# The second cross attention of a perceiver block: context loaded with features over partitions, root and shift spread by transfers

## The reference

```python
def layernorm(t, g, b):
    mu = jnp.mean(t, axis=-1, keepdims=True)
    var = jnp.var(t, axis=-1, keepdims=True)
    return (t - mu) * jax.lax.rsqrt(var + EPS) * g + b
xn = layernorm(x, ln_x_g, ln_x_b)             # x: the context
ln = layernorm(latents, ln_l_g, ln_l_b)
q = ln @ Wq
kv = jnp.concatenate((xn, ln), axis=1) @ Wkv
k, v = jnp.split(kv, 2, axis=-1)
q, k, v = (heads(q) * scale, heads(k), heads(v))
sim = jnp.einsum('bhid,bhjd->bhij', q, k)
sim = jnp.where(mask_full[:, None, None, :], sim, max_neg)
attn = jax.nn.softmax(sim.astype(jnp.float32), axis=-1).astype(sim.dtype)
out = jnp.einsum('bhij,bhjd->bhid', attn, v)
```

## Time and profile before

| | |
|---|---|
| Median of 3 runs | 2112.92 us (2111.11 to 2114.09) |
| The profiled execution | 2115.48 us |
| its span in the profile | 2113.3 us |
| TensorE busy | 1977.3 us, 94% |
| VectorE busy | 1569.6 us, 74% |
| ScalarE busy | 1044.0 us, 49% |
| GpSimd busy | 657.6 us, 31% |
| Mean DMA rate | 50 GB/s |

### The profile page before, as it was taken

The page is one execution under the profiler, slowest core; times in us unless marked ns, Lnnn a source line. Parts: engine busy times, 40 slices in busy tenths (PEclk is TensorE's granted clock), DMA queues, the critical chain, the costliest instruction groups (busy, mean ns, idle before and its releaser), DMA issues. The chain is left out here.

```text
span 2113.3 us, 45029 instructions
## 1 busy us (share of the span) xinstructions
PE 1977.3 (94%) x18290; PEld 1103.7 (52%) x18290; DVE 1569.6 (74%) x2777; ACT 1044.0 (49%) x1484; POOL 657.6 (31%) x696
## 2 busy tenths in 40 slices
PE   7899999999789788999999999999999999888998
PEld 3455555555555443455555555555555555544643
DVE  4689999999857673677777777777777776654676
ACT  2689998998813542333333333333333333323453
POOL 3244444454412230133333322333333322313100
PEclk9899999999799899999999999999999999999999
DMA  4323323322133210000000000000000000210300
GB/s 149 103 54 99 93 65 95 97 64 72 31 142 116 108 41 22 22 23 23 23 4 20 23 23 23 23 23 23 23 2 23 23 23 2 81 46 0 145 21 20
DMA packets 39613, 106.22 MB, mean 50 GB/s; under 512 B 19312, under 2 KB 21616, under 8 KB 33264
## 3 DMA queue, kind: packets, MB, share of 16 engines
q1 hardware_dynamic: 39408, 103.35, 16.1%
HBM read 75.42 MB, written 1.05 MB: 36 GB/s over the span
## 5 line engine op out<-in xcount | busy, mean ns | idle before, releaser
L1468 POOL TENSOR_SCALAR a1c_p_hi<-a1c_pf 128x512 f16<-128x512 f32 x272 | 201.1, 740 | 666.6 <-ACT a1c_pf L1524 624.1
L1326 PE MATMUL PS<-a_x_hi,w_next 128*128 128x512 f16 x1088 | 280.9, 381 | 3.8 <-DVE a1c_v_lo L1598 1.7
L1336 PE MATMUL PS<-w_next,a_x_hi 128*128 128x512 f16 x1088 | 279.0, 379 | 0.0
L1493 ACT ACTIVATE a1c_k_hi<-PS 128x512 f16<-128x512 f32 x136 | 81.2, 597 | 329.4 <-PE PS L1326 329.4
L375 POOL TENSOR_SCALAR a0c_p_hi<-a0c_r 128x1024 f16<-128x1024 f32 x128 | 154.9, 1210 | 268.7 <-DVE a0c_r L475 265.8
L1500 ACT ACTIVATE a1c_v_hi<-PS 128x512 f16<-128x512 f32 x136 | 81.6, 600 | 258.8 <-PE PS L1336 206.0
L480 DVE TENSOR_TENSOR a0c_p_lo<-a0c_r,a0c_p_hi 128x1024 f16<-128x1024 f32 x128 | 201.8, 1576 | 0.9 <-POOL a0c_p_hi L375 0.9
L1673 DVE TENSOR_TENSOR a1c_p_lo<-a1c_pf,a1c_p_hi 128x512 f16<-128x512 f32 x272 | 197.8, 729 | 6.0 <-POOL a1c_p_hi L1468 6.0
L1524 ACT ACTIVATE a1c_pf<-PS,a_maskc 128x512 f32<-128x512 f32 x256 | 175.1, 686 | 49.0 <-PE PS L1835 39.0
L1616 DVE CUSTOM_DVE_ANT_0 a1c_junk<-PS,a1c_maskr 128x512 bf16<-128x512 f32 x256 | 175.9, 687 | 18.8 <-DVE a1c_ctop L1616 0.5
L475 DVE TENSOR_TENSOR a0c_r<-PS,a0c_r 128x1024 f32<-128x1024 f32 x128 | 155.4, 1214 | 32.8 <-ACT a0c_r L421 32.6
(11 more groups left out here) (368 smaller groups left out, 4606.3 us busy)
## 6 DMA issues: line engine op xcount, KB each, us to landing
a_cf<-in_ctxT SPq DMA_DIRECT2D x16, 1024.0 KB, 5.2
a0c_ks<-a0c_k_hi SPq DMA_DIRECT2D x128, 128.0 KB, 2.3
a1c_cf<-in_ctx SPq DMA_DIRECT2D x16, 1024.0 KB, 4.8
a0c_ks<-a0c_k_lo SPq DMA_DIRECT2D x64, 128.0 KB, 2.3
f_w<-in_w SPq DMA_DIRECT2D x4, 1024.0 KB, 8.2
f_w<-in_w SPq DMA_DIRECT2D x1, 4096.0 KB, 20.2
qw_raw<-in_w_gate SPq DMA_DIRECT2D x1, 2816.0 KB, 10.3
qw_raw<-in_w_up SPq DMA_DIRECT2D x1, 2816.0 KB, 11.2
```

The lines of the kernel that those rows point to most:

```text
L1326: mm = nc.tensor.matmul(out, wk[i][:, k, f * P:(f + 1) * P], (x_hi, x_lo)[j][e][:, k, :], start=(step == 0), stop=(step == 11))
L1336: mm = nc.tensor.matmul(out, (x_hi, x_lo)[j][e][:, k, t * P:(t + 1) * P], wv[i][:, k, group * BANK:(group + 1) * BANK], start=(step == 0), ...
L1468: nc.gpsimd.tensor_scalar(p_hi[:, v % 4, :], pf[:, v % 2, :], 1.0, 0.0, ALU.mult, ALU.add)\
```

## The change

The context chunk is now loaded twice: once as before with rows over partitions (`cf`), only for the moments, and once from the transposed copy that the first layer reads too, with *features* over partitions (`ct`, 1 MB, L1406 of the changed file). In `ct` the root and the shift of the normalisation belong to columns, so they have to stand on every partition: SP writes the 2 x 512 numbers `rn` to HBM (`rows_out`, elements of 4 bytes), waits, and reads them back to all 128 partitions (`rows`). VectorE then computes ct x gx x rstd and adds gx x nmr in two instructions for each 128 features (`context_norm`), ScalarE adds the bias and writes the high half `x_hi` directly, VectorE the low half. The transposes, GpSimd's normalising and its high halves are gone; the ring loses its places for the transposes. Moments move to units 1, 2, 4, 5, root and Newton step to unit 6; in the start they move into units 3 to 8.

```diff
-    TURN = UNITS - KT - 1
+    MADE = UNITS - KT - 1
-            if TURN <= v < TURN + KT and j < NCH:
-                RING_ORDER.append(("turn", j, v - TURN))
...
                         if c >= 1:
-                            sp.wait_ge(turned, 4 * c)
+                            sp.wait_ge(stats_done, NT * c)
...
+                        if c >= 1:
+                            sp.wait_ge(x_lo_done, KT * c)
+                        sp.dma_start(ct[:].rearrange("p k n -> p (k n)"), d["ctxT"][c]).then_inc(ct_in, 16)
+
+                    def spread_rows(c):
+
+                        if c >= NCH:
+                            return
+                        sp.wait_ge(newton, 5 * (c + 1))
+                        sp.dma_start(rows_out[c % 2].rearrange("a (t p) -> p a t", p=P), rn[:], allow_slow_non_contiguous=True)\
+                            .then_inc(rows_kept, 16)
+                        sp.wait_ge(rows_kept, 16 * (c + 1))
+                        if c >= 1:
+                            sp.wait_ge(x_done, KT * c)
+                        sp.dma_start(rows[:].rearrange("p a n -> p (a n)"),
+                                     rows_out[c % 2:c % 2 + 1].rearrange("o a n -> o (a n)").broadcast_to([P, 2 * CH]))\
+                            .then_inc(rows_in, 16)
 
...
                     load_context(0)
                     tops(0, 0)
+                    spread_rows(0)
                     load_context(1)
                     for j in range(NJ):
                         tops(j, 1)
+                        spread_rows(j + 1)
                         tops(j + 1, 0)
                         load_context(j + 2)
...
-                    def normalise(c):
-
-                        pool.wait_ge(newton, 5 * (c + 1))
-                        for t in range(NT):
-                            nc.gpsimd.tensor_scalar(cf[:, t, :], cf[:, t, :], rstd[:, t:t + 1], nmr[:, t:t + 1],
-                                                    ALU.mult, ALU.add).then_inc(z_done, 1)
...
-                    normalise(0)
                     mask_row(0)
-                    for k in range(KT):
-                        context_hi(0, k)
...
-                            if j + 1 < NCH and v == 9:
-                                normalise(j + 1)
                             if j + 1 < NCH and v == 11:
                                 mask_row(j + 1)
-                            if j + 1 < NCH and v > TURN:
-                                context_hi(j + 1, v - TURN - 1)
...
-                    def context_f32(c, k):
-                        act.wait_ge(turned, KT * c + k + 1)
-                        if c >= 1 or k >= 2:
-                            act.wait_ge(x_lo_done, KT * c + k - 1)
-                        nc.scalar.activation(xf[:, k % 2, :], g.PS[:, ring_bank("turn", c, k), :], ACT.Identity,
-                                             bias=bx[:, k:k + 1], scale=gx[:, k:k + 1]).then_inc(x_done, 1)
+                    def context_hi(c, k):
+                        act.wait_ge(x_done, KT * c + k + 1)
+                        if c >= 1:
+                            act.wait_ge(v_product, 8 * c)
+                        nc.scalar.activation(x_hi[(c + 1) % 2][:, k, :], ct[:, k, :], ACT.Identity,
+                                             bias=bx[:, k:k + 1]).then_inc(x_hi_done, 1)
...
-                    inverse_root(0)
                     for v in range(UNITS):
                         evacuate(0, v)
-                        if TURN <= v < TURN + KT:
-                            context_f32(0, v - TURN)
+                        if v == 7:
+                            inverse_root(0)
+                        if MADE <= v < MADE + KT:
+                            context_hi(0, v - MADE)
                     for j in range(NJ):
                         for v in range(UNITS):
                             if j + 1 < NJ and v >= 1:
                                 evacuate(j + 1, v - 1)
-                            if j + 1 < NCH and v > TURN:
-                                context_f32(j + 1, v - TURN - 1)
+                            if j + 1 < NCH and MADE <= v < MADE + KT:
+                                context_hi(j + 1, v - MADE)
                             probability(j, v)
-                            if j + 1 < NCH and v == 8:
+                            if j + 1 < NCH and v == 6:
                                 inverse_root(j + 1)
...
-                            dve.wait_ge(z_done, NT * c)
+                            dve.wait_ge(rows_kept, 16 * c)
...
+                    def context_norm(c, k):
+
+                        if k == 0:
+                            dve.wait_ge(ct_in, 16 * (c + 1))
+                            dve.wait_ge(rows_in, 16 * (c + 1))
+                        nc.vector.scalar_tensor_tensor(out=ct[:, k, :], in0=ct[:, k, :], scalar=gx[:, k:k + 1],
+                                                       in1=rows[:, 0, :], op0=ALU.mult, op1=ALU.mult)\
+                            .then_inc(x_scaled, 1)
+                        dve.wait_ge(x_scaled, KT * c + k + 1)
+                        nc.vector.scalar_tensor_tensor(out=ct[:, k, :], in0=rows[:, 1, :], scalar=gx[:, k:k + 1],
+                                                       in1=ct[:, k, :], op0=ALU.mult, op1=ALU.add).then_inc(x_done, 1)
 
                     def context_lo(c, k):
                         dve.wait_ge(x_hi_done, KT * c + k + 1)
                         e = (c + 1) % 2
-                        nc.vector.tensor_tensor(x_lo[e][:, k, :], xf[:, k % 2, :], x_hi[e][:, k, :], ALU.subtract)\
+                        nc.vector.scalar_tensor_tensor(out=x_lo[e][:, k, :], in0=ct[:, k, :], scalar=bx[:, k:k + 1],
+                                                       in1=x_hi[e][:, k, :], op0=ALU.add, op1=ALU.subtract)\
                             .then_inc(x_lo_done, 1)
+
+                    def context_step(c, v):
+
+                        if MADE <= v < MADE + KT:
+                            context_norm(c, v - MADE)
+                        if MADE < v <= MADE + KT:
+                            context_lo(c, v - MADE - 1)
...
-                    for t in range(NT):
-                        moments(0, t)
-                    newton_step(0)
                     for v in range(UNITS):
                         if v >= 1:
                             split_lo(0, v - 1)
+                        if 3 <= v < 3 + NT:
+                            moments(0, v - 3)
+                        if v == 8:
+                            newton_step(0)
                         if v % 2 == 0 and v >= 2:
                             after_period(0, v // 2)
                         if v == 11:
                             new_diag(0, 0)
-                        if v > TURN:
-                            context_lo(0, v - TURN - 1)
+                        context_step(0, v)
...
-                            if j + 1 < NCH and v in (1, 3, 5, 7):
-                                moments(j + 1, (1, 3, 5, 7).index(v))
-                            if j + 1 < NCH and v == 8:
+                            if j + 1 < NCH and v in (1, 2, 4, 5):
+                                moments(j + 1, (1, 2, 4, 5).index(v))
+                            if j + 1 < NCH and v == 6:
                                 newton_step(j + 1)
-                            if j + 1 < NCH and v > TURN:
-                                context_lo(j + 1, v - TURN - 1)
+                            if j + 1 < NCH:
+                                context_step(j + 1, v)
...
-                    def turn(c, k):
-                        bank = ring_bank("turn", c, k)
-                        freed("turn", c, k)
-                        if k == 0:
-                            pe.wait_ge(z_done, NT * (c + 1))
-                        for t in range(NT):
-                            mm = nc.tensor.transpose(g.PS[:, bank, t * P:(t + 1) * P],
-                                                     cf[:, t, k * P:(k + 1) * P], g.ident[:])
-                        mm.then_inc(turned, 1)
...
-                        if TURN <= v < TURN + KT and j < NCH:
-                            turn(j, v - TURN)
```

25 lines of the change are left out of this document (10 added, 15 removed).

## The result

The changed kernel takes **2223.41 us** (median of 4 runs, 2219.51 to 2229.66) against 2113.51 us before (4 runs, 2111.11 to 2117.97): ratio 1.0503, 95% interval 1.0461 to 1.0545. The forecast was 2207 us, range 2168 to 2245. Direction and mechanism came as forecast, the time 16 us higher. The profiled execution of the changed kernel took 2219.51 us with a span of 2217.7, so its span is 104.4 us longer than before, where the prediction said 93.7.

The account below looks back on a forecast made before the run. TensorE, busy 94% of the span, was taken as the bound. Span: 2113.3 - 26.6 - 4.0 + 96.3 + 1.0 + 27 = 2207.0 us, +93.7; on the median 2112.92 that gives 2207 us, range 2168 to 2245.

Parts of the forecast that it names:

- transposes gone, a turn: TensorE in the loop: removing four groups of transposes a chunk saves 1.77 us a turn, 26.6 us in all.
- stall without clock, a turn: TensorE idle ahead of scores 12 (2.7 us) and scores 14 (3.7 us): 6.4 us a turn, 96.3 us in fifteen.
- clock, a turn: Half clock after TensorE's two new pauses: 1.8 us a turn, 27 us in all, bounds 0 to 51 us.
- start, to the first scores: Ahead of the loop: old pause, half clock and transposes go, VectorE waits 2.4 us for rows; gain 4.0 us.
- What bounds the kernel: In the loop TensorE alone sets the 59.54 us turn; what leaves it leaves the time if nobody becomes late.
- Where it lies: VectorE steps 11 to 14: exponentials queue on ScalarE behind context_hi, which waits for context_norm; 6.4 us of stall a turn.
- The price of `context_norm`: On VectorE: two instructions at 0.69 and 0.73 us, 1.42 us until the result is there.
- The rival without loss of clock: TensorE's loop pauses come but the clock stays full: 2180 us; chance 0.20.
- the removal is simply gained: Rival: exponential 11 ends by 7.2 us and the others likewise, so no loop stall: 2082 us; chance 0.06.
- Transfers: SP's write and read-back of root and shift, under 9 us with the issues, stay hidden: cost 0.
- The slack of 15.8 us: Time in a turn from the end of the small steps until VectorE needs the rows: 15.8 us.
- Dearer VectorE: Rival: all eight new VectorE instructions at 0.89 us lengthen the chain 1.6 us a turn: 2231 us; chance 0.11.

Follow-up runs that it names:

- experiment 1: Changed kernel with ScalarE's context_hi moved behind the exponential of the same unit, nothing else: 2179.06 us.
- experiment 7: Changed kernel with context_hi on GpSimd, earlier start, loop moments in units 1 to 4, root and Newton step in 5, context_norm in 10 to 13: 2094.99 us.
- experiment 5: Changed kernel with context_hi made by GpSimd instead of ScalarE, its mask row moved from unit 11 to 10: 2132.34 us.
- experiment 3: Changed kernel with root and shift written as 128 pieces of 32 bytes, context_norm reading and writing at a 32-byte stride: 2260.76 us.
- experiment 8: Changed kernel without context_norm's second instruction, so the shift is not added: 2183.95 us.
- experiment 4: Changed kernel with 40 unused 128x128 products on TensorE ahead of scores 12 and of scores 14: 2205.68 us.
- experiment 2: Kernel before, transposes kept, plus eight VectorE instructions a turn on spare data at context_norm's places, nobody waiting for them: 2140.86 us.
- experiment 6: Changed kernel with an earlier start only: moments in units 1 to 4, root 5, Newton step 6, rows sent ahead of first tops: 2221.10 us.

## Why the prediction was right, and where it was off

Measured against its own sum, all from the two profiled executions (us):

| term | predicted | measured |
|---|---|---|
| transposes gone, a turn | -1.77 | -1.75 |
| stall without clock, a turn | +6.42 | +6.99 |
| clock, a turn | +1.8 | +1.33 |
| late diagonal, a turn | 0 | +0.23 |
| pair 0-1, a turn | 0 | +0.08 |
| fifteen turns (with 1.0 for the first in the forecast) | +97.7 | +103.1 |
| start, to the first scores | -4.0 | +2.2 |
| last two turns | 0 | -2.3 |
| behind the loop | 0 | +1.5 |
| span | +93.7 | +104.4 |

The sum is nearer than its terms, and that is partly luck: the stall came 8.6 us dearer than forecast and the late diagonal 3.4, the clock 7 us cheaper, and the last two turns gave 2.3 back. The largest single miss is the start, 6.2 us and the wrong sign.

*What bounds the kernel.* Right: TensorE set the turn before, and the removal of the transposes is worth 1.75 us a turn when nothing else gets late. The pair 10-11 of experiment 1 shows it (7.23 us with the transposes gone). Experiment 7 realises it: its eight pairs add to 58.5 us on average against 59.47 before, with 0.7 us of new delay left in the last.

*Where it lies.* Right, and the core of the case. Against scores 10 as 0, exponential 11 was put at 9.87 and ended at 10.03, exponential 13 at 20.83 and ended at 21.65, exponential 15 at 27.91 and ended at 28.77. Scores 0 were said to need no wait, and had none. That ScalarE's order is the cause is shown by experiment 1 (move it: 44 us back), experiment 5 (take it off ScalarE: 91 us back, same load on VectorE) and experiments 3 and 8 (make `context_norm` longer or shorter by 3.1 and about 3 us a turn: the turn follows by 3.3 and 2.8).

*The price of `context_norm`.* Mis-sized. The two instructions take 0.746 and 0.752 us and give their result 1.53 us after they begin (1384.58 to 1386.11), not 0.69, 0.73 and 1.42. `context_hi` takes 0.72, not 0.69. Four blocks of this make the 0.57 us by which the stall without clock exceeds its forecast, 8.6 us in fifteen turns. The nearest row was p_lo, a tensor_tensor. It is the operation that makes the difference, not the type: `context_lo` was a tensor_tensor in f32 and f16 of 0.68 us and is now, with the same types, a scalar_tensor_tensor (L1596) of 0.747 us. The low half of the values is a scalar_tensor_tensor too, but reads one operand from PSUM, and takes 0.69 (1387.97).

*The clock.* Right in kind, too large in size: 1.33 against 1.8 us a turn. Both pauses (2.79 and 2.75 us in the turn shown) were put on the same side as those of the earlier trace rows, of 2.61 and 2.56 us. The granted clock fell around the first in thirteen of the fifteen turns, around the second in nine, so not behind every pause. The pair 12-13 is between 11.36 and 11.92 us, the pair 14-15 between 7.22 and 9.52. The rival without loss of clock, 2180 us, is out by experiment 4.

*What VectorE's load does by itself.* Not in the prediction at all. It judged VectorE by who waits at the scores, and said for the rival *the removal is simply gained* that only step 11 and context_hi decide it. Experiment 2 shows a second path, through the PSUM ring and the low half of the values, which costs 25 us with nobody waiting for the new results. In the changed kernel it is hidden, since TensorE stands at the scores anyway; it came out in experiment 2 and, smaller, in experiment 7. So 2082 us could not have been reached without moving VectorE's work too.

*Transfers.* No turn waits for the rows, as forecast, but the step to it was wrong, and the cost is not zero. The write was priced at 2.0 us, the row of a 256 KB output, and takes 9.2 in the start; SP's waits on it average 9.9 us (138.6 / 14). The total was to be under 9 us and is about 14 with the read of 4.4. The slack of 15.8 us (worked out from the start of the last small step, not its end; the write in fact left SP 10.08 us before scores 10) covered that, but not the `tops` behind it: the prediction let them need SP only from -2.5 us on, and by then SP was to be free. It is held until up to 2.4 us after scores 10, and the diagonal waits. Pair 10-11 is 0.23 us a turn over its 10.07, 3.4 us in fifteen, of which 0.8 come from turn 4, where TensorE itself stood for 0.54 us among its score products without a wait that the profile shows. The Trainium skill ("DMA: Bandwidth & Descriptors", Rules for kernel authors) says that a pattern whose last dimension is not contiguous becomes one descriptor for each element, which here would be 1024 a turn. That fits: the page of the changed kernel counts 60861 packets against 39613 before, and in experiment 3, with 128 pieces a turn, 46525. The 14336 fewer are just 16 x (1024 - 128). Experiment 3 shows the pieces to be the cause: 128 pieces of 32 bytes for the same 4 KB land in 1.4 to 1.7 us. Whether their number or their size counts is not separated.

*The start.* Wrong in sign. The step that failed is the wait of 2.4 us for the rows, since it rested on the 2.0 us write; it was 10.01 us, and brought the half clock back that the prediction had counted as gained. With the rows earlier, experiments 6 and 7 start the scores at 869.31 and 866.42 us, 4.6 and 7.5 us ahead of the kernel before: the gain of 4.0 us (forecast bound 7.4) is there once the write is paid early.

*The last two turns.* They gave 2.3 us back, for which the forecast had nothing. The 2.56 us pause of the earlier trace rows at 1834 is 1.04 us after the change. Before, the diagonal ahead of it had waited for the maxima's transfer:

```profile
1832.25 1.04 DVE L1372 TENSOR_TENSOR a1c_diag<-a_ident,a1c_topx 128x512 bf16<-128x512 bf16 x1 [1.55 <-DMA a1c_topx<-a1c_topb]
```

After, it waits 0.37 us, and the half clock that followed the longer pause is gone. Why that transfer landed earlier is open.

*Dearer VectorE.* Did not happen to `context_norm` in the changed kernel, for the reason given (GpSimd's pass follows the exponential and meets other instructions). It happened to the last `context_lo` of fourteen chunks, 1.10 us beside a GpSimd pass, but TensorE was not waiting there. In experiments 1 and 5 it fell on the path.

## What to carry over

Before you move work to an engine, ask who waits for it *in order*, and what is queued behind the waiter: here a result that takes 1.5 us, on an engine with 26% of its time free, cost 5% of the kernel, because the conversion that needed it stood in the same list as the exponentials on which TensorE depends. Moving it one place back in that list gave 44 us, taking it out of the list 91. Place the consumer on an engine in whose queue nothing urgent stands behind it, or make the producer so early that the wait is never met, and check both ends: after that repair the next wait was at the last block's deadline, and after that at the PSUM ring. A transfer of a few KB in a thousand pieces is not a small transfer; price it by its pieces, and ask the same question of it: what is queued behind it.

## What the hardware showed that I had not expected

- A write of 4 KB from SBUF to HBM in 1024 pieces of 4 bytes takes 8.8 to 11.5 us in the changed kernel until the read that waits for it is issued; the same bytes in 128 pieces of 32 bytes land in 1.4 us, 1.7 at most.
- scalar_tensor_tensor of 128x512 with all operands in SBUF: 0.746 to 0.752 us, where one with an operand in PSUM or a tensor_tensor takes mostly 0.68 to 0.69; with f32 operands at a stride of 32 bytes 1.13 us.
- The same instruction begun while a GpSimd pass on SBUF data had 0.56 us to go: 1.10 us. Begun before the pass it kept its 0.75, and the pass took 1.12 in place of 0.69 (experiment 5).
- Around TensorE pauses of 2.5 us and more the granted clock was down in most turns, not in all, and which pair paid for it changed from turn to turn (the last took 7.22 us in one, 8.6 to 9.5 in another). A pause of 2.71 us in the start was followed by products at full pace in experiment 6 (859.38, 1.04 us for four) and at half pace in experiment 7 (856.47, 1.89 us).
